# A fused cross-attention and mixture-of-experts kernel: second pair's down projections scaled by ScalarE and added by transfers

## The reference, cut to what matters

```python
weights = _router_weights(x, Wr, temperature)             # one weight per token and expert
gate = jnp.einsum('btd,edf->ebtf', x, Wg)
up = jnp.einsum('btd,edf->ebtf', x, Wu)
...                                                       # low-rank terms for the first two experts
mid = jax.nn.silu(gate) * up
out = jnp.einsum('ebtf,efd->ebtd', mid, Wd)
...
return jnp.einsum('bte,ebtd->btd', weights, out)
```

## Time and profile before

| | us |
|---|---|
| median of 3 runs | 1072.06 |
| lowest and highest run | 1071.26 and 1073.39 |
| the profiled execution | 1073.63 |
| its span in the profile | 1071.9 |

### The profile page before, as it was taken

The page is one execution under the profiler, slowest core; times in us unless marked ns, Lnnn a source line. Parts: engine busy times, 40 slices in busy tenths (PEclk is TensorE's granted clock), DMA queues, the critical chain, the costliest instruction groups (busy, mean ns, idle before and its releaser), DMA issues.

```text
span 1071.9 us, 12318 instructions
## 1 busy us (share of the span) xinstructions
PE 1045.8 (98%) x4680; PEld 854.1 (80%) x4680; DVE 755.6 (70%) x1278; ACT 443.2 (41%) x631; POOL 54.7 (5%) x60
## 2 busy tenths in 40 slices
PE   6899999999999999999999899999999999999998
PEld 4687878877888888888888788788888888888887
DVE  6889688968485775859487695857658484847654
ACT  4453342555253344435334344534434442524430
POOL 1711122100000000000000010000000000000000
PEclk9999999999999999999999999999999999999999
DMA  9401104145141231514125354311121121111112
GB/s 316 129 15 36 79 9 169 49 129 157 42 142 51 93 108 59 157 60 136 42 98 177 118 157 165 111 40 60 40 79 40 60 60 35 64 39 64 35 40 79
DMA packets 88140, 94.74 MB, mean 88 GB/s; under 512 B 4368, under 2 KB 61840, under 8 KB 87184
## 3 DMA queue, kind: packets, MB, share of 16 engines
q1 hardware_dynamic: 86928, 90.73, 26.5%
q0 software_dynamic: 864, 3.15, 1.0%
q10 hardware_dynamic: 288, 0.07, 0.0%
HBM read 76.63 MB, written 17.30 MB: 88 GB/s over the span
## 4 chain that ended last, share of the span: by engine, by line
PE 80%; DVE 12%; issue 4%; DMA 3%; ACT 1%; SPq 0%; POOL 0%; DVEq 0%
PE gate_up L1557 13%; PE gate_up L1559 13%; PE gate_up L1558 13%; PE tiles L1447 10%; PE tiles L1448 10%; PE tiles L1449 10%; PE gate_up L1515 2%; PE gate_up L1516 2%; PE gate_up L1521 2%; DVE piece_lo L1110 2%; DVE mids_lo L1188 2%; DVE mids L1156 1%; DVE wd_lo L1118 1%; DVE lora_w L1089 1%; PE tiles L1480 1%
## 5 line engine op out<-in xcount | busy, mean ns | idle before, releaser
L1557 PE MATMUL gate_up<-xT_hi,piece_hi 128*128 128x512 f32 x448 | 174.7, 390 | 2.5 <-DVE piece_lo L1110 2.5
L1447 PE MATMUL tiles<-wd_hi,mids_hi 128*128 128x512 f32 x448 | 174.7, 390 | 0.5 <-DVE mids_lo L1188 0.5
L1449 PE MATMUL tiles<-wd_hi,mids_lo 128*128 128x512 f32 x448 | 174.5, 390 | 0.0
L1448 PE MATMUL tiles<-wd_lo,mids_hi 128*128 128x512 f32 x448 | 174.5, 390 | 0.0
L1559 PE MATMUL gate_up<-xT_lo,piece_hi 128*128 128x512 f32 x448 | 174.3, 389 | 0.0
L1558 PE MATMUL gate_up<-xT_hi,piece_lo 128*128 128x512 f32 x448 | 174.3, 389 | 0.0
L1162 DVE SCALAR_TENSOR_TENSOR xacc<-tiles,rw,xacc 128x512 f32<-128x512 f32 x112 | 78.0, 750 | 127.3 <-PE tiles L1449 127.3
L1110 DVE TENSOR_TENSOR piece_lo<-piece,piece_hi 128x1024 fp32r<-128x1024 f32 x112 | 118.1, 1096 | 27.9 <-ACT piece_hi L739 27.9
L1557 PE MATMUL gate_up<-tx_hi,piece_hi 128*128 128x512 f32 x336 | 132.0, 393 | 3.4 <-DVE gates L1143 2.8
L1559 PE MATMUL gate_up<-tx_lo,piece_hi 128*128 128x512 f32 x336 | 131.3, 391 | 0.0
L1558 PE MATMUL gate_up<-tx_hi,piece_lo 128*128 128x512 f32 x336 | 131.3, 391 | 0.0
(11 more groups left out here) (166 smaller groups left out, 1448.7 us busy)
## 6 DMA issues: line engine op xcount, KB each, us to landing
piece<-in_wg_dram SPq DMA_DIRECT2D x40, 256.0 KB, 3.2
piece<-in_wu_dram SPq DMA_DIRECT2D x40, 256.0 KB, 3.4
wd_raw<-in_wd_dram SPq DMA_DIRECT2D x10, 1024.0 KB, 5.1
piece<-merged SPq DMA_DIRECT2D x32, 256.0 KB, 3.2
merged<-lora_w SPq DMA_DIRECT2D x6, 1024.0 KB, 4.2
x_back<-x_spill SPq DMA_DIRECT2D x9, 512.0 KB, 5.3
w_raw<-in_xT_dram SPq DMA_DIRECT2D x4, 1024.0 KB, 6.2
wd_raw<-merged SPq DMA_DIRECT2D x4, 1024.0 KB, 5.6
```

The lines of the kernel that those rows point to most:

```text
L1447: nc.tensor.matmul(dst, w_h, x_h, start=first, stop=False)
L1448: nc.tensor.matmul(dst, w_h, x_l, start=False, stop=False)
L1449: return nc.tensor.matmul(dst, w_l, x_h, start=False, stop=last)
L1557: nc.tensor.matmul(dst, w_h, x_h, start=first and kt == 0, stop=False, skip_group_check=True)
```

## The change

In steps 8 to 13 (the down projections of steps 7 to 12, those of the second pair but for the last) VectorE's two `add_down` are left out. In their place ScalarE runs `scale_down(k-1, h)`: four ACTIVATE instructions of 128x512, each of which multiplies one bank of `tiles` by the per-partition weight from `rw` and writes it into a tile of a new buffer `staged` (in the SBUF of the first pair's sums, stored by then). Each increments `d_added`. GpSimd waits for that and issues a transfer that adds the staged tile into `xacc` (`accum_op=ALU.add`), SBUF to SBUF, 256 KB each, eight a step and 48 in all. The first half's scalings stand after `copy_u2(j + 1)` and ahead of `piece_high_part(j + 3)`, the second half's after `copy_u2(j + 2)` and ahead of `piece_high_part(j + 4)`. GpSimd rather than VectorE now waits for `acc_loaded`. VectorE still does the adding in steps up to 7 and at the end (step 13's own projections), where it first waits for all transfers.

```diff
...
         lora_a_split, lora_b_hi, lora_b_lo = (at(name, kb, [P, S], f32r) for name, kb in
                                               (("lora_a_split", 26), ("lora_b_hi", 30), ("lora_b_lo", 28)))
 
+        staged = at("staged", 0, [P, 2 * TT, D])
         x_back = at("x_back", 16, [P, 4, 2 * S])
 
 
...
         mids_lo_made = sem("mids_lo_made")
         d_mm = sem("d_mm")
         d_added = sem("d_added")
+        staged_added = [sem(f"staged_added{i}") for i in range(2 * TT)]
         merged_stored = sem("merged_stored")
 
 
...
             load_again(1, 2, 3)
             load_again(0, 2, 2)
 
+            def add_staged(k, h):
+                for t in range(TT):
+                    i = h * TT + t
+                    pool.wait_ge(d_added, 8 * k + i + 1)
+                    pool.dma_start(tile_of(2 + h, t), staged[:, i, :], accum_op=ALU.add).then_inc(staged_added[i], 16)
+
+            pool.wait_ge(acc_loaded, 16)
+            for k in range(SWAP, STEPS - 1):
+                for h in range(2):
+                    add_staged(k, h)
+
 
         @block.scalar
         def _(act):
...
                 act.wait_ge(mids_made, 8 * k + 4 * m + c + 1)
                 h, f = 1 if c in (C12, C22) else 0, m if c in (C12, C11) else m + 2
                 nc.scalar.activation(mids_hi[h][:, f, :], mids[h][:, f, :], ACT.Copy).then_inc(mids_hi_made, 1)
+
+            def scale_down(k, h):
+
+                s = 1 + k % SWAP
+                for t in range(TT):
+                    i = h * TT + t
+                    act.wait_ge(d_mm, 8 * k + i + 1)
+                    if k == SWAP:
+                        act.wait_ge(stored, 16 * 2 * TT)
+                    else:
+                        act.wait_ge(staged_added[i], 16 * (k - SWAP))
+                    col = ((2 + h) * TT + t) * E + s
+                    nc.scalar.activation(staged[:, i, :], tiles[:, t, :], ACT.Copy, scale=rw[:, col:col + 1]).then_inc(d_added, 1)
 
             t_high_part(tx_hi[:, 1, :], tx_sum[:, 1, :], 1)
             t_high_part(tx_hi[:, 0, :], tx_sum[:, 0, :], 4)
...
                     copy_p1(j + 1)
                     copy_p5(j + 1)
                     copy_u2(j + 1)
+                    if k > SWAP:
+                        scale_down(k - 1, 0)
                     piece_high_part(j + 3)
                     for c in (C12, C11, C22, C21):
                         gate_silu(k, 1, c)
...
                     copy_p1(j + 2)
                     copy_p5(j + 2)
                     copy_u2(j + 2)
+                    if k > SWAP:
+                        scale_down(k - 1, 1)
                     piece_high_part(j + 4)
                     wd_high_part(k)
                 mid_high_part(k, 0, C12)
...
                     if k == SWAP - 1:
                         back_sum(0, 1, 4)
                         back_sum(2, 3, 4)
-                    if k == SWAP + 1:
-                        dve.wait_ge(acc_loaded, 16)
-                    add_down(k - 1, 0)
+                    if k <= SWAP:
+                        add_down(k - 1, 0)
                     piece_sums(j + 3)
                     if k == SWAP - 1:
                         back_sum(1, 3, 6)
...
                         difference(x_back[:, 0, :], x_back[:, 3, :], x_back[:, 0, :])
                         dve.wait_ge(t_made, 6)
                         difference(x_back[:, 3, :], x_back[:, 3, :], x_back[:, 1, :])
-                    add_down(k - 1, 1)
+                    if k <= SWAP:
+                        add_down(k - 1, 1)
                     if lora:
                         lora_a_low_part(k)
                         lora_b_low_part(k)
...
             mid_low_part(k, 1, C22)
             make_mid(k, 1, C21)
             mid_low_part(k, 1, C21)
+            for i in range(2 * TT):
+                dve.wait_ge(staged_added[i], 16 * (STEPS - 1 - SWAP))
             add_down(k, 0)
             add_down(k, 1)
 
```

## The result

The changed kernel is slower: 1085.74 us median (1083.6 to 1089.33), the kernel before on the same chip 1071.66; the ratio is 1.0132, 95% interval 1.0101 to 1.0163. The prediction was 1084.7 us, in a range of 1077.5 to 1089.5. The profiled execution took 1086.71 us (predicted: 1086.2), and its span is 1085.0. By the medians the loss is 14.1 us, where 12.6 were forecast; by the interval of the ratio it lies between some 10.8 and 17.5 us, so the medians alone would not tell these two apart.

What follows compares the result with a forecast made beforehand. TensorE was taken as the bound, so relieving VectorE gains nothing; ScalarE's scalings make TensorE wait, 6 x 0.84 plus 5 x 1.51 us, 12.6 in all, giving 1072.06 + 12.6 = 1084.7 us, range 1077.5 to 1089.5.

Steps and rivals of the forecast that it cites:

- The bound: Steps 8 to 13: TensorE works all the time, so removing 36 us of VectorE additions is worth nothing.
- X: Time that a bunch of four scalings occupies on ScalarE: 4 x 0.59 = 2.36 us, ends 1.96 and 2.76.
- Stretch A: Middle of steps 8 to 13, behind the first four scalings: late combine C22 delays TensorE by X - 1.52, 0.84 us.
- Stretch B: From the second four scalings into the next step, steps 8 to 12: TensorE delayed by X - 0.85, 1.51 us.
- The slacks: Time a bunch may take before TensorE is delayed: 1.52 us in Stretch A, 0.85 us in Stretch B.
- 11 X - 13.37: Total loss, 6 x (X - 1.52) + 5 x (X - 0.85): 12.6 us with X = 2.36.
- Step 13: Second four scalings there: no piece is rounded, so a 0.5 us delay of C12 is absorbed.
- The transfers: 256 KB each, about 4.0 us, nobody else waits for them before the end: no cost even at double the length.
- GpSimd's issues: Four issues of 0.74 us behind the scalings end before VectorE's low part; overlap only if an issue takes over 1 us.
- the rival: GpSimd's issues hold VectorE's next instruction at each bunch: 8.1 us more, to 1092.8 us; chance 0.11.

Runs made afterwards that it cites:

- both bunches moved: Changed kernel with the first half's scalings behind the rounding of piece j+3 and the second half's behind copy_u2 of quad j+3: 1072.73 us, ratio 0.9993.
- the run with C22 ahead: Changed kernel with VectorE's combine C22 of quad j+1 ahead of the low part of piece j+3 from step 8 on: 1078.74 us, ratio 1.0051.
- the three points of the table: Changed kernel with 256 of 512 columns scaled and transferred, with a constant scale, and as is: 3.2, 8.3 and 12.5 us over before from step 8.
- constant scale: Changed kernel with scalings by a constant in place of the column of router weights: 1082.25 us, ratio 1.0075.
- second bunch moved: Changed kernel with only the second half's scalings moved, to behind copy_u2 of quad j+3: 1078.11 us, ratio 1.0045.
- the sum was moved away: VectorE's x_back sum in step 6 put behind combine C22: 1069.14 us on the kernel before, 1069.03 us on the changed kernel with both bunches moved.

## Why the prediction was right

- **The bound.** TensorE was full in steps 8 to 13, and taking work from VectorE bought nothing: with both bunches moved the time is that of before (0.9993).
- **X.** Predicted 2.36 us with ends 1.96 and 2.76, measured 2.28. A scaling lasts 0.69 us, as the read with a bias column did, and the next starts 0.57 us after it where 0.59 was taken. The overlap is 0.12 us rather than 0.10 to 0.11. So an operand per partition was the right likeness; a scale held in the instruction comes to 0.48 us.
- **Stretch A.** Predicted 0.84 us, measured 0.80, six times. The waits in TensorE's list are 0.5 us each where 0.6 was said. The way through VectorE was shown by the run with C22 ahead.
- **Stretch B.** Predicted 1.51, measured 1.50, five times; the waits for `mids` in the list are 0.6 us each where 0.8 was said. The delay passes through fourteen instructions without loss, and none is made up.
- **The slacks.** With the measured X the sum 11 X - 13.37 gives 11.7 us where 12.5 were found: A and B come out 0.04 and 0.07 us larger than X - 1.52 and X - 0.85. For A the trace has the reason: the rounding right behind the scalings lasts 1.73 us in place of 1.70, with transfers or without, and 1.70 again where the scalings were moved away. For B the way from the bunch to product 4's second matmul is as the sum says (814.08 - 796.78 = 17.30); 0.06 us lie ahead of it, since the bunch comes 14.13 us after A's second matmul in place of 14.07. X, 0.08 too large, hid all that (11 x 0.08 = 0.9). The closeness of the total, 12.6 against 12.5, is partly this luck; the three points of the table show that the two thresholds and the growth with X hold on their own, to 0.07 us a stretch.
- **Step 13.** It was predicted to absorb its second bunch, and the profile has five waits for `mids`, not six.
- **The transfers.** Predicted at no cost. A transfer took 5.2 us against the 4.0 of the earlier trace rows, and the kernel without them loses 12.3 of the 12.5 us. That nobody else waits for them is right for the changed kernel and was luck of the place in part: alone, issued beside the load of the down weights, they made that load 2 us longer and cost 1.0 us from step 8 on.
- **GpSimd's issues.** Here the prediction's sum was off, though not its outcome. It lets four issues of 0.74 us end 0.7 us after the last scaling and sees an overlap with VectorE's low part from issues of over 1 us on. With its own numbers the first scaling ends at 0.69, four issues end at 0.69 + 4 x 0.74 = 3.65, which is 1.2 us after the last scaling (2.46), and the low part starts at 4.09, so the overlap begins at (4.09 - 0.69) / 4 = 0.85 us an issue. They took 0.87 us each, and it did begin. In the changed kernel's step 9:

```profile
776.50 3.48 POOL L592 DMA_DIRECT2D xacc<-staged  x4 [37.46 <-ACT staged L799]
```

  That is until 779.98. ScalarE's rounding ended at 779.53 and VectorE's low part, which reads two operands in SBUF, started at 779.56, 0.03 us behind it as where no issue runs, and inside the last issue. The pair of them took 2.09 us, as everywhere. So the rival's condition was met and its cost was not: no hold of VectorE in 0.4 us of overlap. The rule of the Trainium skill (SBUF — State Buffer, SBUF: two separate sides) is for a GpSimd operation that reads SBUF, and no run here shows that the issue of a transfer is one; the prediction took it for one when it said that by that rule the rival would come true.

What the prediction left out is the spread outside these steps: the changed kernel with and without its transfers differs by 0.2 us from step 8 on, but by 3.1 us in the spans of the two profiled executions. Of these, 3.0 come up in step 6, as the last section tells.

## What to carry to other kernels

Before work is moved to an idle engine, read what stands behind its new place in that engine's order and who waits for it: the loss here was the length of the insert less the slack of that one chain, and each slack could be read from the trace to within 0.1 us. Work put behind the last thing that the full engine waited for was free here; the first bunch, one instruction earlier, cost 0.8 us a step, and the second, ahead of three roundings, 1.5. Transfers that nobody waits for can still delay a load that somebody does, so look which loads are in flight when they are issued. Relief of an engine that isn't the bound was worth nothing, and an unrelated wait of the bounding engine, found in the same list of waits, was worth more.

## What was not expected of the hardware

Of the ten traces that have the wait in step 6, some show a fall of TensorE's clock behind it. The stretch from 585 to 600 us of the kernel before and then of the changed kernel without transfers (length, PE, PEld, DVE, ACT, POOL, clock, DMA share, GB/s):

```profile
585.00:600.00 15.00, 12.20 (x48) 9.59 (x47) 11.57 (x15) 4.76 (x6) 0.00 (x0) 0.89 0.49 165
```

```profile
585.00:600.00 15.00, 13.24 (x59) 10.62 (x57) 10.88 (x13) 5.02 (x7) 0.00 (x0) 1.00 0.54 181
```

Behind the 2.80 us wait of the kernel before, seven matmuls start 0.43 us apart, the lower of the clock's two levels (1.2 GHz), before the spacing of 0.23 us returns at 599:

```profile
596.06 0.63 PE L1559 MATMUL gate_up<-tx_lo,piece_hi 128*128 128x512 f32 x1
596.49 0.63 PE L1557 MATMUL gate_up<-tx_hi,piece_hi 128*128 128x512 f32 x1
```

Waits of 2.3 us (both bunches moved), 2.4 (C22 first), 2.8 (before) and 3.2 (changed) had such a fall, with 0.89 to 0.92 in the window. Five others, of 1.7 to 1.9 us, stayed at 1.00. One of 1.8 us (constant scale) had it nonetheless, so the length of the wait alone doesn't decide. Two runs price the fall: with a wait of 1.78 us and the fall, step 6 lasts 54.47 us (constant scale), and with a wait of 1.77 us and no fall 52.84 (second bunch moved), so the fall costs 1.6 us. A wait of TensorE can thus cost more than its length. Step 6 lasts 52.7 to 53.0 us in the five without the fall and 54.5 to 55.8 in the five with it. This is most of why spans differ by up to 3 us between kernels that are equal from step 8 on, and why the ratios above are less exact than the stretches from step 8; the rest lies ahead of step 6, which starts between 559.2 and 561.6 us in the twelve traces, and was not followed up. Which execution gets the fall stays open. Where the sum was moved away the clock in this window is 1.00.
